# A node embedding is projected once and transposed on TensorE; ScalarE copies the transposed tile

## What is computed

```python
xn = _layernorm(x, axis=-1)                    # 6250 x 256
z = xn @ W_P_w + W_P_b                         # W_P_w: 256 x 128
embeds = z + W_pos                             # 6250 x 128
q = (rowE @ qT)   # rowE = embeds[rows]; k, v of colE = embeds[cols] likewise
...
out = agg + embeds                             # embeds is needed again here
```

## Time and profile before

| | before |
|---|---|
| median of 3 runs | 7137.58 us (7130.84 to 7146.11) |
| the profiled execution | 7143.9 us, its span 7142.2 us |
| TensorE busy in the span | 5250.5 us (74%) |
| VectorE | 5435.4 us (76%) |
| ScalarE | 3467.9 us (49%) |
| GpSimd | 4755.4 us (67%) |
| `enter`: first product (582.16) to last kv copy's end (681.22) | 99.06 us |

### The profile page before, as it was taken

One profiled execution on the slowest core, in us unless ns is written; L12 is line 12 of the kernel. 1 busy time (PEld: TensorE's weight loads), 2 busy tenths in 40 slices (PEclk: granted clock), 3 DMA queues, 4 the chain that ended last, 5 costly groups with the idle time before them and its releaser, 6 DMA issues. The chain is left out here.

```text
span 7142.2 us, 115844 instructions
## 1 busy us (share of the span) xinstructions
PE 5250.5 (74%) x28073; PEld 4112.7 (58%) x28073; DVE 5435.4 (76%) x15728; ACT 3467.9 (49%) x9814; POOL 4755.4 (67%) x5326
## 2 busy tenths in 40 slices
PE   5995776767677777566666666666679999999781
PEld 3664555556566666355556555665446666666671
DVE  7984777678888888677777777777767777777776
ACT  0002766765555555566666666666322222222561
POOL 1441777777777776577777777776367777777781
PEclk7557898887777777888887888787568888888555
DMA  1006454544444444454544545444423322232447
GB/s 28 4 4 148 135 138 137 141 133 122 121 124 120 121 121 117 115 138 132 139 132 132 137 132 138 132 131 118 109 51 60 64 59 59 60 64 57 124 121 192
DMA packets 502711, 769.39 MB, mean 108 GB/s; under 512 B 119802, under 2 KB 365657, under 8 KB 502061
## 3 DMA queue, kind: packets, MB, share of 16 engines
q0 software_dynamic: 198048, 441.63, 23.9%
q1 hardware_dynamic: 292961, 308.36, 15.9%
q10 hardware_dynamic: 11052, 12.00, 0.7%
HBM read 689.74 MB, written 71.83 MB: 107 GB/s over the span
## 5 line engine op out<-in xcount | busy, mean ns | idle before, releaser
L706 POOL DMA_INDIRECT att_kv_e<-kv,gnn_idx x3240 | 3111.7, 960 | 1199.7 <-issue 964.2
L791 PE MATMUL att_ps_sum<-att_vals,att_hot 128*125 128x136 f32 x6480 | 1246.6, 343 | 1156.6 <-DVE att_vals L849 599.9
L791 PEld LDWEIGHTS att_ps_sum<-att_vals,att_hot 128*125 128x125 f32 x6480 | 1042.6, 231 | 1400.4 <-DVE att_vals L849 737.7
L706 POOL DMA_INDIRECT max_rows<-rows,gat_idx x1128 | 1068.2, 947 | 423.9 <-issue 337.3
L866 DVE TENSOR_TENSOR acc<-acc,att_ps_sum 125x136 f32 x3240 | 951.8, 294 | 381.0 <-DVE acc L866 72.6
L777 PE MATMUL att_ps_q<-qs,att_hot_t 125*128 x6480 | 1146.7, 335 | 90.3 <-ACT att_hot_t L823 78.6
L777 PEld LDWEIGHTS att_ps_q<-qs,att_hot_t 125*128 125x128 f32 x6480 | 1067.4, 248 | 124.7 <-issue 123.4
L808 ACT ACTIVATE att_hot<-node_no,gnn_loc 128x125 f32<-128x125 f32 x3240 | 1014.3, 384 | 0.0
L2432 DVE CUSTOM_DVE_ANT_0 max_junk<-max_far,max_ps_b 125x256 bf16<-125x256 bf16 x2256 | 792.3, 415 | 261.1 <-PE max_ps_b L2396 261.1
L801 ACT ACTIVATE att_ps_dve<-att_clipped 128x32 f32<-128x32 f32 x810 | 162.4, 200 | 1430.1 <-DVE att_clipped L857 1429.2
L836 DVE TENSOR_TENSOR att_prod<-att_ps_q,att_kv_e 128x512 f32<-128x512 f32 x810 | 553.3, 683 | 379.5 <-DMA att_kv_e<-kv,gnn_idx 142.2
(11 more groups left out here) (454 smaller groups left out, 7966.7 us busy)
## 6 DMA issues: line engine op xcount, KB each, us to landing
att_local<-gnn_loc_rows SPq DMA_DIRECT2D x810, 128.0 KB
att_kv_e<-kv,gnn_idx POOLq DMA_INDIRECT x3240
max_local<-gat_loc_rows SPq DMA_DIRECT2D x282, 128.0 KB
gs_local<-gat_loc_rows SPq DMA_DIRECT2D x141, 256.0 KB, 3.3
outs<-ex_y SPq DMA_DIRECT2D x25, 896.0 KB
max_rows<-rows,gat_idx POOLq DMA_INDIRECT x1128
X<-in_x SPq DMA_DIRECT2D x10, 1120.0 KB
ans_late<-outs SPq DMA_DIRECT2D x11, 896.0 KB
```

The source lines that it names most:

```text
L706: pool.indirect_dma_start(rows(j, e), None, source, bass.IndirectOffsetOnAxis(ap=g.idx[:, t:t + 1], axis=0))\
L791: ins = pe.matmul(sum_of(u, i), hot[:, g_of % SLOTS, e, :], vals[:, g_of % VALS, e, :], start=True, stop=True)
```

## The change

The second product is gone, and with it the bias row on all partitions, its two loads and VectorE's addition. Instead TensorE transposes the finished `ET` tile (`turn_back`, after `project`) into the same place in `ps_e`, and ScalarE copies it to `E` (`e_out`, after `copy_kv`). `et_out(t)` waits in addition for the transpose of t-2, which reads the `ET` buffer that it writes. The wait of `times_w(t)` for `e_out(t-2)` is as it was.

```diff
-        bias, pos = sb("bias", [NODE_TILE, D]), sb("pos", [NODE_TILE, D])
...
-            def e_out(t, h):
-                dve.wait_ge(m["projected"], t + 1)
-                dve.tensor_tensor(E[:, t], e_ps(h), bias[:], ALU.add).then_inc(m["e_out"], 1)
-
             def et_out(t, h):
                 dve.wait_ge(m["projected"], t + 1)
                 wait(dve, m["qkv"], t - 1)
+                wait(dve, m["turned_back"], t - 1)
...
-                    dve.wait_ge(m["w_in"], 16 * 8)
-                    chain(dve.tensor_tensor(bias[:], bias[:], pos[:], ALU.add))
+                    dve.wait_ge(m["w_in"], 16 * 6)
                     dve.tensor_tensor(bias_col[:], bias_col[:], pos_col[:], ALU.add).then_inc(m["w_ready"], 1)
...
                     et_out(n, n % 2)
-                    e_out(n, n % 2)
...
                 wait(pe, m["e_out"], t - 1)
                 wait(pe, m["et_out"], t - 1)
                 for ch in range(KC):
-                    pe.matmul(et_ps(h), wp[:, ch, :], xT[:, t % TURNED, ch, :], start=ch == 0, stop=ch == KC - 1)
-                for ch in range(KC):
-                    ins = pe.matmul(e_ps(h), xT[:, t % TURNED, ch, :], wp[:, ch, :], start=ch == 0, stop=ch == KC - 1)
+                    ins = pe.matmul(et_ps(h), wp[:, ch, :], xT[:, t % TURNED, ch, :], start=ch == 0, stop=ch == KC - 1)
                 ins.then_inc(m["projected"], 1)
...
+            def turn_back(t, h):
+                pe.wait_ge(m["et_out"], t + 1)
+                pe.transpose(e_ps(h), ET[:, h, :], c.ident[:]).then_inc(m["turned_back"], 1)
...
                     project(n - 1, (n - 1) % 2)
+                    turn_back(n - 1, (n - 1) % 2)
...
-            load_row(act, bias[:], ins["L0_gnn_W_P_b"], m["w_in"])
-            load_row(act, pos[:], pos_row, m["w_in"])
...
+            def e_out(t, h):
+                act.wait_ge(m["turned_back"], t + 1)
+                act.copy(E[:, t], e_ps(h)).then_inc(m["e_out"], 1)
...
                     copy_kv(n - 1, (n - 1) % 2)
+                    e_out(n - 1, (n - 1) % 2)
             act.wait_ge(m["q_copied"], tiles)
+            act.wait_ge(m["e_out"], tiles)
```

More of the change, by code:

```diff
@@ L1823, in enter @@
                                       "root_ready", "scales", "normed", "turned", "turned_sb", "projected", "e_out",
-                                      "et_out", "qkv", "q_copied", "kv_copied"])
+                                      "et_out", "turned_back", "qkv", "q_copied", "kv_copied"])
         saved = st.enter_context(semaphores(nc, [f"enter_saved{n}" for n in range(TURNED)]))
```

## The result

The changed kernel takes 7161.7 us, the median of 6 runs (7156.6 to 7171.8), against 7137.2 for the kernel before in 6 runs (7130.8 to 7146.1). The ratio is 1.0037, with a 95% interval of 1.0024 to 1.0049: slower, by 17 to 35 us. The forecast was 7161, the range 7148 to 7180.

The account below looks back on a forecast made before the run. TensorE was taken to bound stage enter. Terms of +21.8 (long stretch), +0.7 (first tiles), +2.4 (clock rise) and -1.5 us (start) summed to +23.4, giving a forecast median of 7161 us, range 7148 to 7180.

Parts of the forecast that it names:

- long stretch, 46 periods: Main part of stage enter at full clock: period 2.35 us in place of 1.88, +21.8 us in all.
- first three periods: Start of enter at half clock: 2.10 and twice 3.69 us, 9.5 against 8.77, so +0.7 us.
- further delay of the clock's rise: Enter beyond the first tiles: 6.5 us more at the lower clock level, +2.4 us, bounds 0 and 11.
- start: Before TensorE's first work in enter: one addition and two row loads fewer, -1.5 us, between 0.3 and 3.0 won.
- The chain: Per tile in enter: project, qs, kv and E copies, product and turn close a period of 2.35 us (2.27 to 2.48).
- The chunk ends: Every ten tiles in enter: without VectorE's addition, the mean excess of 0.06 us per period should go.
- The clock: TensorE in enter: clock rises 16 us after the first product, twice what it takes now, and the higher level then holds.
- The copy's price: ScalarE's 128-column copy in enter: 0.27 us by the trace; the skill's 0.41 would add 0.14 per period, some 6.5 us.
- The first: Chain doesn't close, TensorE stays the bound: 7117 us, if E copy ends by P + 0.76 (P: project's start); 3%.
- The second: Clock stays low through all of enter because of TensorE's gaps of 0.55 us per tile: +82, 7220 us; 8%.
- the third: Chain closes but tighter: copies 0.17 apart, clock rises right away, 3 us won at the start: +16, 7153 us; 13%.
- The signs: Enter's changed profile: period 2.35, E-copy wait about 0.7 us, clock 0.50 for 10 to 40 us, first transpose 1-2 us earlier.

Follow-up runs that it names:

- moved_copy: Kernel before, both products kept, with E's copy moved from VectorE to ScalarE behind the qs and kv copies, without its bias; ratio 1.0066.
- vector_copy: Changed kernel with the E copy on VectorE, behind et_out, instead of on ScalarE; ratio 1.0013.
- copied_twice: Changed kernel with the E copy made twice on ScalarE, first into an unused tile, then into E; ratio 1.0049.
- start_only: Kernel before without the bias row's two loads and VectorE's first addition, E copied by VectorE without its bias; ratio 1.0007.
- ring: Changed kernel with two PSUM banks of its own for the transposed tile, two banks for project's result and five kv_sb buffers, not two; ratio 0.9976.
- own_banks: Changed kernel with the transposed tile in two PSUM banks of its own, so the product no longer waits for the E copy; ratio 0.9989.
- copy_first: Changed kernel with the transpose put ahead of project on TensorE and the E copy ahead of the qs and kv copies on ScalarE; ratio 0.9988.
- removed_only: Changed kernel without the added transpose, the E copy and the waits for both, E filled with zeros by GpSimd; ratio 0.9996.

## Why the prediction was right

The terms, against the traces of before and after:

| term | forecast | measured |
|---|---|---|
| long stretch, 46 periods | +21.8 | 109.94 - 86.31 = +23.6 |
| first three periods | +0.7 | 8.24 - 8.81 = -0.6 |
| further delay of the clock's rise | +2.4 | 0, see below |
| start | -1.5 | 579.35 - 581.05 = -1.7 |
| last product to last kv copy's end | not counted | 3.51 - 3.94 = -0.4 |
| sum | +23.4 | +20.9 |

The fourth product of the kernel before starts at 590.97, 0.04 after the window of the earlier trace rows ends, hence 8.81. That 7161 us was met within 1 us is in part luck. The chain was put 1.8 us too low and the two terms of the clock together 3.7 too high, and these errors cancel by half. The profiled executions then differ by 20.6 us and the medians by 24.5: runs of one kernel scatter by more than the forecast missed.

**The chain.** Its form was right in each link, and moved_copy, vector_copy and copied_twice, whose periods were forecast by it at 2.83, 2.07 and 2.57, came out at 2.83, 2.08 and 2.56. The period was mis-sized by 0.04 us: 0.84 + 0.16 + 0.27 + 0.28 + 0.10 + 0.52 + 0.22 = 2.39. The kv copy is followed by the next after 0.27, where the copy of xT gave 0.25, and the copy's end to the product's start is 0.10, where I took 0.05 from the earlier trace rows; part of it came back in the product, 0.52 in place of 0.55.

**The chunk ends.** They went, as stated: in the changed kernel all 46 periods are 2.39. In vector_copy, which puts a copy back on VectorE, they are there again (2.57 once in ten).

**The clock.** This step failed, and its direction with it. I took a rise 16 us after the first product, later than before, because TensorE stops once per tile. It rose after 5.5 us, with TensorE busy for 4.76 of 5.54 us; in the kernel before, after 7.6, with 7.18 of 7.64. Over all eleven traces the delay is 4.9 to 8.1 us, and 5.1 to 6.1 in the four whose product waits for the E copy, so no delay by the gaps shows. The first three periods took 2.09, 3.76 and 2.39 us, where 2.10 and twice 3.69 were forecast: the chain at the lower level was sized well, but the third period ran at the higher one, and nothing was left for the term behind it. That the higher level then holds was right: 1.00 through 69% busy time.

**The start.** Right in size (1.5 us over ten traces): the load is still waited for, for 1.36 us in place of 2.70. Its parts were not right: the last load is issued 1.76 us earlier and not 0.96 (start_only).

**The copy's price.** E's copy takes 0.285 us on ScalarE. The estimate of 0.41 from the Trainium skill (page "ScalarE: Activation LUTs", section "Rules for kernel authors") would have made the period 2.5; the trace disagrees with it. The page's budget is for an ACTIVATE, and E's copy is a COPY; an ACTIVATE of the same stage, on 10 columns, took 0.30 (changed kernel, 641.78).

**The rivals.** The first, TensorE as the bound at 1.42, failed at exactly the point named: the E copy would have to end before P + 0.76, and it ends at P + 1.55. ring shows that it is what happens once both chains are open. The second, the clock low all stage, didn't come. Of the third, the early rise of the clock came, but the kv and E copies started 0.27 apart and not 0.17 (3.7 us of its 7.6), and the start gave 1.7 us and not 3.0.

**The signs.** The E copy 0.27 behind the kv copy, the earlier first transpose and the wait of 0.7 us per tile came as forecast; xT is waited for 0.9 us in all. Two signs failed: the wait list doesn't name ScalarE's E copy but "issue", and the clock stood at 0.50 for 5.5 us and not for 10 to 40.

## What to carry to other kernels

A step taken from the bounding engine is worth its time only if the result of its substitute is read before that engine comes to the buffer again. Lay one period out as a chain of starts and compare it with the engine's own work: here 2.39 against 1.42. Ahead of giving more memory, look at what stands in the queue before the releasing instruction; two lines in another order were worth as much as two more banks. And when one chain is opened, work out the next before the run: it was 1.60, not 1.42, until project had a second bank as well.

## What was not expected of the hardware

- The granted clock rises 4.9 to 8.1 us after the first product in all eleven traces, with TensorE busy for 86% to 94% of that time; the late stage of the earlier trace rows stays at 0.50 with 90%. What tells the two apart wasn't tried.
- project (384 columns in f32) needs mostly 0.84 or 0.85 us to ScalarE's waiting copy where it starts 0.11 us behind the record before it, and 0.92 where it starts 0.18 us behind or later (own_banks, copy_first, removed_only).
- A VectorE `tensor_scalar` on 125 x 10 elements takes 2.15 us in all eleven traces, beside GpSimd's fill of `acc`, and another 4.73 us beside the fill of E in removed_only. Both end within 0.04 us behind the fill, while TENSOR_TENSOR operations of that size take 0.17 or 0.18 beside it.
